# The first loads of a one-core kernel: a transposed input cut in a quarter and a rest, seven small loads moved from SyncE's queue to ScalarE's

## The reference, cut to what matters

```
x = x + pooled(x)      # scores = tanh(x W1 + b1) . v ; masked softmax of the scores, by type
                       # (prefix, postfix or all but itself) ; weighted mean over x, divided by the count
x = x + stencil(x)     # zX * lap_x + zY * lap_y + zR * x * (1 - x)
x = x + adapter(x)     # weights of the profile number: relu(x Wd + bd) Wu + bu, + x, layer norm
x = x + temporal(x)    # context scan, gate, two decaying traces, blend, three 512 x 512 products,
                       # layer norm
```

## Time and profile before

| | us |
|---|---|
| median of 3 runs | 690.57 |
| the profiled execution | 691.58 |
| its span | 689.8 |
| TensorE busy in it | 652.3 (95%) |
| VectorE busy | 551.5 (80%) |
| ScalarE busy | 370.0 (54%) |

### The profile page before, as it was taken

How to read it: one execution, slowest core, us unless ns; L and a number is a source line. 1 busy time by engine, 2 the same in 40 slices (tenths; PEclk the granted TensorE clock), 3 DMA queues, 4 the chain that set the end, 5 groups by cost and what they waited for, 6 DMA issues and landing times.

```text
span 689.8 us, 8219 instructions
## 1 busy us (share of the span) xinstructions
PE 652.3 (95%) x2848; PEld 491.8 (71%) x2848; DVE 551.5 (80%) x792; ACT 370.0 (54%) x759; POOL 176.1 (26%) x268
## 2 busy tenths in 40 slices
PE   3989989899899999999999999999999999999996
PEld 1545444477677878787878787888787878787875
DVE  2685877869997998799879987998799749974955
ACT  1143368666476357635764576357635743574244
POOL 5003412211065025411441154114411210121001
PEclk9999999999999999999999999999999999999999
DMA  6988999996048844562456335634463320031001
GB/s 205 329 304 287 269 248 313 335 342 163 0 56 156 152 64 100 119 95 54 101 133 104 60 94 116 96 62 98 111 97 61 50 74 0 1 56 68 1 0 61
DMA packets 51575, 86.83 MB, mean 126 GB/s; under 512 B 8256, under 2 KB 10304, under 8 KB 51406
## 3 DMA queue, kind: packets, MB, share of 16 engines
q0 software_dynamic: 16896, 33.56, 30.5%
q1 hardware_dynamic: 31134, 52.74, 21.3%
q10 hardware_dynamic: 3504, 0.01, 0.3%
HBM read 63.22 MB, written 22.04 MB: 124 GB/s over the span
## 4 chain that ended last, share of the span: by engine, by line
PE 60%; DVE 22%; ACT 7%; issue 6%; DMA 3%; SPq 1%; POOLq 0%; POOL 0%; ACTq 0%; DVEq 0%
PE bank L1177 16%; PE bank L1178 16%; PE bank L1179 16%; DVE tr L1750 5%; PE bank L1074 3%; DVE tr L1741 2%; ACT mod L855 2%; DVE wgb L1737 2%; DMA xts<-in_xT 2%; PE bank L1173 2%; DVE wgb L1729 2%; PE bank L1253 2%; DMA beside_scratch<-xts 1%; DVE tr L1758 1%; ACT wgb L868 1%
## 5 line engine op out<-in xcount | busy, mean ns | idle before, releaser
L1750 DVE TENSOR_TENSOR_SCAN tr<-alpha,carry,tr 128x512 f32<-128x512 f32 x48 | 58.9, 1267 | 0.0
L642 POOL TENSOR_TENSOR rs_a<-ss_a,consts 128x1 f32<-128x1 f32 x32 | 16.0, 499 | 143.3 <-ACT junk_f L822 143.0
L1177 PE MATMUL bank<-th,wg_l 128*128 128x512 f32 x128 | 51.9, 406 | 0.0
L1177 PE MATMUL bank<-xh,wg_l 128*128 128x512 f32 x128 | 51.9, 406 | 0.0
L1178 PE MATMUL bank<-xl,wg_h 128*128 128x512 f32 x128 | 50.5, 394 | 0.0
L1178 PE MATMUL bank<-tl,wg_h 128*128 128x512 f32 x128 | 50.5, 394 | 0.0
L1179 PE MATMUL bank<-xh,wg_h 128*128 128x512 f32 x128 | 50.2, 392 | 0.0
L1179 PE MATMUL bank<-th,wg_h 128*128 128x512 f32 x128 | 50.2, 392 | 0.0
L874 ACT ACTIVATE carry<-tr 128x2 f32<-128x2 f32 x32 | 6.6, 206 | 80.3 <-DVE tr L1750 80.3
L1737 DVE SCALAR_TENSOR_TENSOR wgb<-wgb,soma 128x512 f32<-128x512 f32 x32 | 22.0, 687 | 30.5 <-ACT wgb L868 30.5
L602 POOL TENSOR_TENSOR late_side_f<-x2b 128x510 f32<-128x510 f32 x24 | 28.3, 1177 | 56.8 <-DMA x2b<-x_scratch 26.1
(11 more groups left out here) (290 smaller groups left out, 2011.3 us busy)
## 6 DMA issues: line engine op xcount, KB each, us to landing
x2b<-beside_scratch POOLq DMA_DIRECT2D x12, 1024.0 KB, 9.1
xr<-rows_scratch POOLq DMA_DIRECT2D x10, 1024.0 KB, 10.2
xb<-in_x SPq DMA_DIRECT2D x8, 1024.0 KB, 14.6
result<-xr SPq DMA_DIRECT2D x7, 1024.0 KB, 4.3
beside_scratch<-xts SPq DMA_DIRECT2D x6, 1024.0 KB, 11.2
x2b<-rows_scratch POOLq DMA_DIRECT2D x6, 1024.0 KB, 10.9
x_scratch<-xb SPq DMA_DIRECT2D x5, 1024.0 KB, 13.0
x2b<-x_scratch SPq DMA_DIRECT2D x5, 1024.0 KB, 5.5
```

Of the source, the lines that this page charges most:

```text
L642: po.tensor_tensor(rs[:, c:c + 1], ss[:, c:c + 1], eps, ALU.add).then_inc(chain, 1)
L1177: pe.matmul(acc, wl, xh_, start=start, stop=False)
L1750: ve.tensor_tensor_scan(t[:, d], alpha[:, 1 + d:2 + d].broadcast_to([P, GN]), t[:, d], 0.0 if first else carry[:, k, 1 + d:2 + d], ALU.mul ...
```

## The change

Three things are changed. `xT(0,0)` comes as two transfers, the first 128 of its 512 channels under the old semaphore and the other 384 under `xt0_rest`; TensorE waits for the second ahead of the second product of `hidden(0,0)`. The seven small loads leave SyncE's stream and stand ahead of the 11 on ScalarE's, `v` first, so that `xT(0,1)` follows right behind `xT(0,0)`. And the waits are split: TensorE starts with W1 alone (`w1_in` at 16) and waits for `v_set` at `scores(0,0)`; ScalarE and VectorE wait for `bv_in` at 32.

```diff
                         sp.dma_start(w1_sb[:], w1.rearrange("(k p) a -> p k a", p=P)).then_inc(w1_in, 16)
-                        load_xt(0, 0)
-                        sp.dma_start(b1_sb[:], col(b1)).then_inc(w1_in, 16)
-                        sp.dma_start(v_sb[:], col(v)).then_inc(w1_in, 16)
-                        for dst, src in ((typ_i[:], ptype), (coef[:, 0], zx), (coef[:, 1], zy),
-                                         (coef[:, 2], zr)):
-                            sp.dma_start(dst, row(src, P)).then_inc(coef_in, 16)
-                        sp.dma_start(ids[:], profile.rearrange("(o n) -> o n", o=1)).then_inc(ids_in, 16)
+                        xT_0 = xT[0:1].rearrange("o (k p) t -> p (o k) t", p=P)
+                        sp.dma_start(xt_slot[0][0][:, 0:1], xT_0[:, 0:1, 0:GN]).then_inc(xt_in[0][0], 16)
+                        sp.dma_start(xt_slot[0][0][:, 1:], xT_0[:, 1:, 0:GN]).then_inc(xt0_rest, 16)
...
+                        act.dma_start(v_sb[:], col(v)).then_inc(bv_in, 16)
+                        act.dma_start(b1_sb[:], col(b1)).then_inc(bv_in, 16)
+                        for dst, src in ((typ_i[:], ptype), (coef[:, 0], zx), (coef[:, 1], zy),
+                                         (coef[:, 2], zr)):
+                            act.dma_start(dst, row(src, P)).then_inc(coef_in, 16)
+                        act.dma_start(ids[:], profile.rearrange("(o n) -> o n", o=1)).then_inc(ids_in, 16)
                         load(taus[:, 0:1], row(tau_ctx, P))
...
-                    act.wait_ge(w1_in, 48)
+                    act.wait_ge(bv_in, 32)
                     tanh(0, 0)
...
+                            if n == 0 and k == 1:
+                                pe.wait_ge(xt0_rest, 16)
...
+                        if n == 0:
+                            pe.wait_ge(v_set, 1)
...
-                    pe.wait_ge(w1_in, 48)
-                    pe.wait_ge(v_set, 1)
+                    pe.wait_ge(w1_in, 16)
                     hidden(0, 0)
...
-                    ve.wait_ge(w1_in, 48)
+                    ve.wait_ge(bv_in, 32)
                     ve.tensor_copy(v_rep[:], v_sb[:].broadcast_to([P, P])).then_inc(v_set, 1)
```

More of the change, by code:

```diff
@@ L354, in build_program @@
             w1_in = sem("w1_in")
+            bv_in = sem("bv_in")
+            xt0_rest = sem("xt0_rest")
             v_set = sem("v_set")
```

## The result

| | before | after |
|---|---|---|
| median | 690.65 (4 runs, 690.47 to 690.93) | 698.44 (4 runs, 697.66 to 700.46) |
| profiled execution | 691.58 | 697.66 |
| its span | 689.8 | 695.9 |

The ratio is 1.0103, with a 95% interval of 1.0084 to 1.0121: 7.8 us slower by the medians, 6.1 by the two profiled executions. The forecast was 692.6 us; its direction holds, its size doesn't, and 697.0, the end of the range, was passed. The rest is the scatter of the changed kernel: its profiled execution is the fastest of the four, with a mean granted clock of 0.991, and the other three have 0.988 or 0.989. TensorE probably loses more to its clock in them; no trace shows where.

The account below looks back on a forecast made before the run. TensorE was taken as the bound, winnable only in the first 17.1 us, which hang on `xT(0,1)`. The loads' -3.8 us, taken back by ScalarE, become +2.0, clock 0: 690.57 to 692.6 us, range 688.6 to 697.0.

Parts of the forecast that it names:

- TensorE's clock: TensorE standing some 5 us before `scores(0,0)` might slow its clock: 0 to 1.8 us more, taken as 0.
- ScalarE's hold: ScalarE's held issues end at 20.5 us, so `scores(0,0)` starts at 22.6 and not 20.63: 2.0 us later.
- late bound of 930: ScalarE's last load issued at the latest with 930 packets of its queue outstanding, at 23.3 us.
- The loads' 3.8 us: In the head, earlier landings of `xT(0,0)` and `xT(0,1)` end `hidden(0,1)` at about 17 us, 3.8 us ahead.
- The parameters: `params_in` lands at about 29.3 us, before 19.8; column products of `scores(0,3)` start at 33.8, the time they have now.
- the prediction's own 4.5 us: Time from the landing of `params_in` to the start of the column products of `scores(0,3)`: 4.5 us.
- the holds don't add: Of the waits for ScalarE's issues and for `params_in` only the later counts, named as the first, +2.0 us.
- The shift reached the end: A shift of the head reaches the kernel's end in full; a difference over 1 us means this step failed.
- Only issue time moves over: Rival: ScalarE's 18 issues end at 16.2 us, `scores(0,0)` starts at 18.3, 2.3 us faster, 688.3 us; chance 0.21.
- the two holds come out even: Rival: ScalarE free at 18.5 us, `params_in` at 29.3, the loads' gain just eaten, 690.6 us; chance 0.30.
- The queue stands behind the big loads: Rival: ScalarE's last four loads each wait 2.7 us for a SyncE megabyte; free at about 25 us, 697.6; chance 0.12.

Follow-up runs that it names:

- the five products: Changed kernel with five extra, unused TensorE products between `hidden(0,1)` and `scores(0,0)`: 694.90 us, ratio 1.0049.
- The split alone: Changed kernel with its seven small loads back on SyncE's queue, behind the two parts of `xT(0,0)`: 692.17 us, ratio 1.0016.
- Move only: Changed kernel with `xT(0,0)` in one transfer again, the seven small loads still on ScalarE: 698.16 us, ratio 1.0099.
- the first hold is dodged: Changed kernel with `tanh(0,0)` ahead of the last four loads in ScalarE's stream: 703.02 us, ratio 1.0158.
- the parameters late: Changed kernel with `tanh(0,0)` ahead of ScalarE's last four loads and everything that waits for the parameters placed later: 691.91 us, ratio 0.9999.

## Why the prediction was wrong

- **The step that failed is TensorE's clock.** The prediction saw that TensorE would stand, took 0 for the clock, and kept 1.8 us for the range. It measured 3.5 (3.47 between the same two rows before and after, 3.46 by the five products). I sized it by one start from rest, 5.34 against 3.54 us. But those 1.8 us are the half pace of only four of the eight records of that block. Behind a stop the array stayed at half for nearly 7 us, which reached over `scores(0,0)` and most of `hidden(0,2)`. Both my ends were too low: the row that I bounded it by shows the same pace, a record every 0.86 us, for half as long. The other row, 2.6 us of idle time for 0.16, was taken as the nearer in kind and was not.
- **ScalarE's hold was right in kind, and 0.6 us short.** Forecast: the last issue at 20.5 us, `scores(0,0)` at 22.6. It was 21.08 and 23.20, +2.57 for +2.0. Its two working numbers were off and nearly cancelled: the queue drained more slowly (953 packets through by 12 us where 171 a us from 4.9 give 1,500), and the last issue was let go with 4,370 - 2,578 = 1,790 packets outstanding, where I used some 1,400. My late bound of 930 was misread too: counted in one stretch, 2,552 packets were through by 11.55 us in the kernel before, which leaves 808. And no single number of outstanding packets fits all the issues, as said above.
- **The loads' 3.8 us never came.** `hidden(0,1)` ended at 20.61 and not at 17: the rest landed at 11.5 us where I had 8, and TensorE, started early and stopped, did the first seven of 14 records at half pace. The split alone costs some 1 us, where I had put it inside the sum with a gain; and `zr` landed at 13.95 us and not by 10 to 12, which nothing waited for long. In the changed kernel this cost nothing, since ScalarE was later still. Move only has the lead (16.4 us) and ends at the same time.
- **The parameters.** Forecast 29.3 us with a gate even with before; they landed at 32.98. With the prediction's own 4.5 us behind them the column products couldn't have started before 37.5, +3.7 us, where the first hold alone would give 33.78 + 2.57 = 36.35. So the holds don't add, as said, but the wrong one was named the later. An estimate from these: without the fall of the clock, the changed kernel would have been held at 37.5, and the clock's part net of that is 2.3 us. That the wait for the parameters is real is shown where the first hold is dodged (703.02 us) and where both are (691.91).
- **The shift reached the end** in the changed kernel: +6.03 at `block_sums`, +6.1 in the span. It doesn't in every kernel here: with eleven loads on GpSimd the two differ by 1.5 us.
- **The rivals.** "Only issue time moves over" and "the two holds come out even" fell by ScalarE's last issue at 21.08 us. "The queue stands behind the big loads", 697.6 at a chance of 0.12, came closest in time, but by another way: ScalarE was free at 21 us and not at 25, and its packets weren't shut out, since small and big ones went one for one. Only its price for one issue, 2.7 us, was near (2.47, 2.84 and 2.88). The Trainium skill's sentence on issue time (DMA: Bandwidth & Descriptors, "Issuing engines are not separate DMA queues") doesn't cover this: what moved over was not issue time but waiting in it.

## What to carry to other kernels

An issue took half a us in some places of these kernels and 2.5 to 2.9 us in others. In an engine's stream it is a wait like any other, and the computation behind it pays. Before moving a load off a queue that "only issues", count the packets of the queue that it is moved to, and look what that engine must do next. When a wait makes TensorE stand, price it twice, the wait and the half-speed stretch that can follow it, and look whether the next wait in line is hidden by the first.

## What the hardware showed that I had not expected

- Small loads over 128 partitions issued by GpSimd come as far fewer packets: on ScalarE's queue q10 all 18 are 4,370. With the last four on GpSimd, q10 carries 2,642 and GpSimd's queue q0 128 more than before; with eleven there q10 has 866 and q0 352 more.
- The granted clock reads 1.00 in the first 17 us of the changed kernel, though up to 16.8 us its records start 0.86 us apart, as they do later at a clock of 0.50, and then 0.43 us apart. The slow start shows in the records alone.
- The kernels differ in where the head stands, and several have a stretch at half clock near 75 to 92 us that the profiled execution of before lacks (0.57 from 88 to 92 us with the parameters late). Ahead of TensorE's wait for `xb` it costs nothing, as in the changed kernel; behind it, with eleven loads on GpSimd and with the parameters late, it costs some 1.5 us, which is as much as most of these edits move.
